# Moving side work in a fused attention and MLP kernel: weight signs in halves, one norm later, one y block a step, weight sums at the heads of steps

## The reference

```python
q = _l2norm(proj(Wq)); k = _l2norm(proj(Wk)); v = proj(Wv)
attn = jnp.einsum('bhqd,bhkd->bhqk', q, k)
mask = (rel < 0) | (rel >= WINDOW)              # rel = key - query, WINDOW = 128
bias = jnp.where(mask, NEG_INF, -abs(rel) * slopes)
attn = jax.nn.softmax(attn + bias, axis=-1)
out = einsum('bhqk,bhkd->bhqd', attn, v) @ Wo.T
x = _layernorm(x + out)                          # called y below
# MLP: bw = mean(|w|, axis=1) * sign(w)
h = gelu(x @ bw1.T + b1)
x = _layernorm(x + h @ bw2.T + b2)
```

## Time and profile before

| | |
|---|---|
| median of 3 runs | 389.81 us (389.2 to 392.25) |
| the profiled execution | 391.93 us, its span 390.2 us |
| granted TensorE clock, mean | 0.99 of full |
| busy: PE, DVE, ACT, POOL | 372.1, 303.2, 311.3, 273.9 us |

### The profile page before, as it was taken

How to read it: one execution, slowest core, us unless ns; L and a number is a source line. 1 busy time by engine, 2 the same in 40 slices (tenths; PEclk the granted TensorE clock), 3 DMA queues, 4 the chain that set the end, 5 groups by cost and what they waited for, 6 DMA issues and landing times.

```text
span 390.2 us, 12067 instructions
## 1 busy us (share of the span) xinstructions
PE 372.1 (95%) x3921; PEld 239.8 (61%) x3921; DVE 303.2 (78%) x856; ACT 311.3 (80%) x533; POOL 273.9 (70%) x418
## 2 busy tenths in 40 slices
PE   8788999999999999999999899999999999999992
PEld 5544665666566656665666556666666666666671
DVE  3965767776777677767777787765899999999985
ACT  2687788878887888788878878868998888888774
POOL 1185888888888888788877998869556646655221
PEclk9998999999999999999999999999999999999997
DMA  7596555653355335533553448420522124304113
GB/s 235 118 247 144 119 127 108 149 123 82 81 121 120 82 81 120 121 81 81 122 119 82 82 85 134 83 55 5 54 55 55 55 55 110 89 19 108 55 54 108
DMA packets 98544, 38.30 MB, mean 98 GB/s; under 512 B 84688, under 2 KB 97360, under 8 KB 98256
## 3 DMA queue, kind: packets, MB, share of 16 engines
q1 hardware_dynamic: 98512, 37.89, 44.1%
HBM read 12.72 MB, written 4.19 MB: 43 GB/s over the span
## 4 chain that ended last, share of the span: by engine, by line
PE 78%; DVE 8%; issue 4%; ACT 3%; POOL 2%; DMA 2%; SPq 1%; DVEq 0%; POOLq 0%; ACTq 0%
PE ps L506 14%; PE ps L377 13%; PE ps L540 13%; PE ps L366 12%; PE ps L348 8%; PE ps L388 6%; PE ps L411 6%; PE ps L396 3%; PE ps L403 2%; DVE ss L894 1%; DMA qkT<-parts 1%; POOL parts L1263 1%; PE ps L451 1%; ACT prob L639 1%; POOL prob L1243 1%
## 5 line engine op out<-in xcount | busy, mean ns | idle before, releaser
L1243 POOL TENSOR_SCALAR_AFFINE_SELECT prob<-prob 128x512 f32<-128x512 f32 x252 | 153.5, 644 | 19.4 <-ACT prob L639 19.4
L639 ACT ACTIVATE prob<-ps 128x1024 f32<-128x1024 f32 (+1 forms) x128 | 123.0, 1014 | 0.4 <-PE ps L348 0.3
L377 PE MATMUL ps<-wqkv,xt 128*128 128x512 f32 x128 | 72.9, 657 | 1.9 <-DVE qkn L911 1.9
L506 PE MATMUL ps<-yT,sgn 128*128 128x512 f16 x256 | 61.2, 379 | 0.0
L540 PE MATMUL ps<-sgn,prob 128*128 128x256 f16 x512 | 60.6, 273 | 0.2 <-DVE prob L1042 0.2
L705 ACT ACTIVATE ps<-ps,bias,alpha 128x512 f32<-128x512 f32 x64 | 47.7, 754 | 13.3 <-PE ps L506 10.3
L540 PEld LDWEIGHTS ps<-sgn,prob 128*128 128x128 f16 x512 | 50.0, 98 | 12.2 <-DVE prob L1042 0.5
L1309 POOL TENSOR_TENSOR resid<-z,resid 128x256 f32 (+1 forms) x31 | 22.5, 726 | 45.1 <-DVE z L1052 45.1
L366 PE MATMUL ps<-prob,vdiag 128*17 128x128 f32 x1024 | 51.2, 274 | 1.6 <-POOL prob L1243 1.6
L366 PE MATMUL ps<-prob,vnext 128*17 128x128 f32 x992 | 49.8, 273 | 0.0
L843 DVE COPY parts<-parts 128x512 f16<-128x512 f16 x32 | 19.7, 615 | 35.0 <-POOL parts L1263 34.9
(11 more groups left out here) (108 smaller groups left out, 580.5 us busy)
## 6 DMA issues: line engine op xcount, KB each, us to landing
xt<-in_xT SPq DMA_DIRECT2D x32, 128.0 KB, 2.4
resid<-in_x SPq DMA_DIRECT2D x32, 128.0 KB, 2.3
out_dram<-resid SPq DMA_DIRECT2D x7, 512.0 KB, 3.0
w_t<-in_w2T SPq DMA_DIRECT2D x1, 1024.0 KB, 7.9
w_t<-in_w1T SPq DMA_DIRECT2D x1, 1024.0 KB, 6.5
w_nat<-in_w SPq DMA_DIRECT2D x4, 256.0 KB, 3.6
wqkv<-in_wqkvT SPq DMA_DIRECT2D x3, 256.0 KB, 3.9
qkT<-parts SPq DMA_TRANSPOSE x32, 4.3
```

The source lines that it names most:

```text
L377: mm = nc.tensor.matmul(ps[:, QK[1 - par], :], xt[:, slot, k, :], wqkv[:, k, 0:2 * D], start=(k == 0), stop=(k == DC - 1))
L506: mm = nc.tensor.matmul(ps[:, bank, :], sgn1[:, c, P * k:P * k + P], yT[:, par, a, c, :, :], start=(m == 0), stop=(m == 2 * DC - 1))
L639: nc.scalar.activation(to, scored, ACT.Exp, scale=QK_SCALE ** -2).then_inc(exp_done, 1)
L1243: return nc.gpsimd.affine_select(out=at, in_=at, compare_op=ALU.is_ge, fill=0.0, base=-near, pattern=[[0, CH], [1 if near else -1, P]], ch ...
```

## The change

Nothing is computed differently. On ACT, `signs1` becomes two halves of 128 x 1024 in the asides of steps 2 and 3, behind exponential 3, and waits for the w1T load alone. `norm_of(0)` leaves the end of step 0 and stands in step 1 behind exponential 1. The first group's four high_y go one each into steps 24 to 27; the second group's go one each into 28 and 29, and two into 30. In step 29 the high halves move from behind exponential 1 to behind exponential 3. On POOL the first group's four low_y go one each into steps 24 to 27, ahead of the low halves. On DVE `fade_values(1, 1)` leaves step 1 and stands in step 0 ahead of the Newton round of block 3; the second 128 columns of the w2 sums become two pieces of 64 at the very heads of steps 2 and 3; the w1 sums and the two bound pieces move from the asides to the heads of steps 24 to 27, ahead of the doubling copy. On SP and PE the order is the same, only the semaphores that are waited for are renamed or counted anew (`turn_y(0, 0)` still stands between the transposes of blocks 28 and 29).

```diff
@@ sync
-            sp.dma_start(w1_t[:], w1T).then_inc(mlp_in, 16)
+            sp.dma_start(w1_t[:], w1T).then_inc(w1t_in, 16)
...
-                sp.dma_start(dst[:], src).then_inc(mlp_in, 16)
+                sp.dma_start(dst[:], src).then_inc(bias_in, 16)
@@ scalar: step()
                 exps(0)
                 exps(1)
-                if early2:
+                if amid:
+                    amid()
+                if high_behind == 1:
                     high_halves(i, par)
...
                 exps(3)
+                if high_behind == 3:
+                    high_halves(i, par)
                 if aside:
                     aside()
-                if next3 or prev3:
+                if norm and (next3 or prev3):
                     norm_of(i, next3, prev3)
...
-            def signs1():
-                act.wait_ge(mlp_in, 16 * 3)
-                nc.scalar.activation(sgn1[:], w1_t[:], ACT.Sign).then_inc(sgn_ready, 1)
+            def signs1(part):
+                act.wait_ge(w1t_in, 16)
+                nc.scalar.activation(sgn1[:, part], w1_t[:, part], ACT.Sign).then_inc(sgn_ready, 1)
...
-            step(0, 0, prev2=False, prev3=False, early2=True, both=False)
-            step(1, 1, prev2=False, prev3=False)
-            signs1()
-            step(2, 0, prev3=False)
-            step(3, 1)
+            step(0, 0, prev2=False, prev3=False, high_behind=1, both=False, norm=False)
+            step(1, 1, prev2=False, prev3=False, amid=lambda: norm_of(0, True, False))
+            step(2, 0, prev3=False, aside=lambda: signs1(0))
+            step(3, 1, aside=lambda: signs1(1))
...
-            step(NB - 8, 0, aside=lambda: high_pair(0))
-            step(NB - 7, 1, aside=lambda: high_pair(2))
-            step(NB - 6, 0, aside=lambda: high_y(1, 0, 1))
-            step(NB - 5, 1, aside=lambda: high_y(1, 1, 1))
-            step(NB - 4, 0, aside=lambda: high_y(1, 2, 1))
-            step(NB - 3, 1, next3=False, early2=True, aside=lambda: high_y(1, 3, 1))
-            step(NB - 2, 0, next2=False, next3=False)
+            step(NB - 8, 0, aside=lambda: high_y(0, 0, 0))
+            step(NB - 7, 1, aside=lambda: high_y(0, 1, 0))
+            step(NB - 6, 0, aside=lambda: high_y(0, 2, 0))
+            step(NB - 5, 1, aside=lambda: high_y(0, 3, 0))
+            step(NB - 4, 0, aside=lambda: high_y(1, 0, 1))
+            step(NB - 3, 1, next3=False, high_behind=3, aside=lambda: high_y(1, 1, 1))
+            step(NB - 2, 0, next2=False, next3=False, aside=high_pair)
@@ vector: step()
+                if ahead:
+                    ahead()
                 if cur and not next3:
                     fade_values(i, par)
                 if next1:
...
+            def second_block():
+
+                double(2, 0)
+                fade_values(1, 1)
...
-            step(0, 0, prev2=False, next1=False, prev3=False, prev4=False, aside=lambda: abs_w2(0),
-                 amid=lambda: double(2, 0))
-            step(1, 1, prev2=False, next1=False, prev3=False, prev4=False)
...
-            step(2, 0, prev3=False, prev4=False, aside=abs_w2_and_residuals)
-            dve.wait_ge(mlp_in, 16 * 3)
+            step(0, 0, prev2=False, next1=False, prev3=False, prev4=False, aside=lambda: abs_w2(0, P), amid=second_block)
+            step(1, 1, cur=False, prev2=False, next1=False, prev3=False, prev4=False)
+            step(2, 0, prev3=False, prev4=False, ahead=lambda: abs_w2(P, P + P // 2),
+                 aside=lambda: dve.wait_ge(first_resid, 16 * XS))
+            dve.wait_ge(bias_in, 16 * 2)
...
-            step(3, 1, prev4=False)
+            step(3, 1, prev4=False, ahead=lambda: abs_w2(P + P // 2, D))
...
-            step(NB - 8, 0, aside=lambda: abs_w1(0))
-            step(NB - 7, 1, aside=lambda: abs_w1(1))
+            step(NB - 8, 0, ahead=lambda: abs_w1(0))
+            step(NB - 7, 1, ahead=lambda: abs_w1(1))
...
-            step(NB - 6, 0, aside=bound_sides)
-            step(NB - 5, 1, aside=bound_rows)
+            step(NB - 6, 0, ahead=bound_sides)
+            step(NB - 5, 1, ahead=bound_rows)
@@ gpsimd
+                if before_low:
+                    before_low()
                 if next2 and not early2:
                     low_halves(i, par)
...
-            for b in range(GB):
-                step(NB - 8 + b, b % 2)
-                if b < 2:
-                    low_y(0, 2 * b, 0)
-                    low_y(0, 2 * b + 1, 0)
+            step(NB - 8, 0, before_low=lambda: low_y(0, 0, 0))
+            step(NB - 7, 1, before_low=lambda: low_y(0, 1, 0))
+            step(NB - 6, 0, before_low=lambda: low_y(0, 2, 0))
+            step(NB - 5, 1, before_low=lambda: low_y(0, 3, 0))
```

More of the change, by code:

```diff
@@ L622, in take_rows, with step @@
                                      ACT.Copy).then_inc(ot_ready, 1)
-            def step(i, par, prev2=True, next2=True, next3=True, prev3=True, early2=False, both=True,
-                     rows_first=False, aside=None):
+            def step(i, par, prev2=True, next2=True, next3=True, prev3=True, high_behind=None, both=True,
+                     rows_first=False, norm=True, amid=None, aside=None):
                 if prev2:
@@ L938, in _, with abs_w2 @@
             nc.vector.tensor_copy(vnext[:, :, HD], fade[:, 1, :]).then_inc(consts, 1)
-            def abs_w2(part):
-                cols = slice(part * P, part * P + P)
+            def abs_w2(first, last):
+                cols = slice(first, last)
                 dve.wait_ge(w2_in, 16)
```

26 lines of the change are left out of this document (12 added, 14 removed).

## The result

| | before | after |
|---|---|---|
| median of the runs | 390.00 us (9 runs) | 388.27 us (9 runs, 387.05 to 388.76) |
| the profiled execution, its span | 391.93, 390.2 us | 388.27, 386.4 us |
| ratio of the times | | 0.9945 (0.9925 to 0.9965) |

The medians differ by 1.7 us (0.44%); the ratio of all the runs says 0.55%, with an interval of 0.35 to 0.75%. The forecast was 382.8 us, a gain of 7, in a range of 381.0 to 386.0. The two profiled executions differ by more than the medians do, 3.7 against 1.7 us; that difference is the first thing to explain.

A forecast was written before the change was run, and what follows sets the result against it. PE was taken as the bound, so only overlong steps could give: 0.9 + 3.70 - 0.2 + 2.68 - 0.2 + 0.4 = 7.3 us; carried to the median 382.5, named 382.8 us, range 381.0 to 386.0.

The forecast's parts named there:

- What bounds the kernel: PE is busy throughout a plain step of 7.75 or 7.76 us; only longer steps can give anything.
- Signs in halves: Step 2 falls from 11.45 to 7.75 us: gain 3.70, of which 1.57 strips wait and about 1.7 half clock.
- The first rival: Step 2: the clock falls all the same, or didn't in the median's runs; 1.7 us not gained, 384.5; chance 0.12.
- Norm of block 3: Step 1: exponentials and masks start earlier, gain 0.9 us (0.54 to 1.22); later qkn of block 3 costs 0.
- The landing: Start of step 3: transpose of block 3 lands at 36.5, close to need; charged 0.2 us, bounds 0 and 0.5.
- w2 pieces: Heads of steps 2 and 3: each piece fits DVE's 1.38 us wait for POOL's low halves; cost 0, bound 0.3.
- w1 sums, high_y, low_y: Steps 25 and 26 return to 7.76 us: gain 1.64 + 1.04 = 2.68 us, lower bound 1.06.
- The contention: Step 25: low_y beside DVE's Newton round delays the w1 sum; charged 0.2 us, bounds 0 and 1.1.
- the second rival: Side work only moves its stall: sign halves hold norms, or y transpose holds block 29's; either 384.6 us; chance 0.15.
- Step 29: High halves behind exponential 3 end PE's 0.68 us wait for oT; gain 0.4 us, bounds 0 and 0.68.
- SP and the y transpose: End of step 27: transpose of y ready about 3.5 us later, closer to block 29's; taken as 0.
- the signs of being wrong: qkT wait at step 3 or 29, otok wait in 3 or 4, clock 0.50 past 20 us, slow Newton operations in 24-27.

The follow-up runs named there:

- norm_back: The changed kernel with the norm of block 3 back at the end of step 0 and the fades back in step 1: 388.04 us, ratio 0.9927.
- before_again: The unchanged kernel from before the change, measured and profiled once more: 390.26 us, ratio 1.0002.
- late_only: Kernel before with only the late half of the change (y, w1 sums, bounds, step 29); steps 0 to 3 as before: 389.28 us, ratio 0.9970.
- high_first: The changed kernel with ACT's high halves of block 3 ahead of the norm of block 4 in step 1: 388.22 us, ratio 0.9942.

## Why the prediction was wrong

*What bounds the kernel.* Right: PE does, and step 26 fell to 7.79 us, step 2 in norm_back to 7.75.

Two steps of it failed, each by about 1.8 us: the size of the signs' term, and the cost of the moved norm, which was put at 0. A third, the landing of block 28 in step 27, was no term at all and cost 0.9.

*Signs in halves, 3.70 us.* The mechanism was right (the wait for strips is gone), but the size came from one execution: "about 1.7 the half clock" was in the profiled run of before and not in its usual one (9.69 against 11.45 us). The gain to be had was 1.94 us by before_again, and 1.45 by late_only, where the bias load came sooner. The first rival, which said just this, was given 0.12. The sign was in the numbers: the profiled execution lay 2.1 us above the median, and the text carried that over as a constant, but for 0.3 us, instead of asking which term it was in. The Trainium skill (TensorE: Matmul & The Clock Gate, Part 1) says that the monitor behind the clock runs free of the kernel's start, so that a fall comes at other places in other runs; the two profiles of one kernel agree, 0.50 and 1.00 in the same half microsecond.

*Norm of block 3: gain 0.9, cost 0.* The gain was about right (0.74 us). "Cost 0" failed as a mechanism. It argued that the high halves wait for the norm of block 4 anyway, and took that norm's time as given; but its seed stands on DVE behind the Newton round that was moved, and the move put the round beside POOL's masks, 1.75 us for its three operations instead of about 0.6. The cost was 0.86 us by the wait for otok and its like (step 2 at 8.61 or 8.62 where block 3 lands in 4.6 us, against 7.75). Where it lands slowly, step 2 is 9.60 us against 8.29 with the norm back: 1.31. No run took POOL's masks away from that round alone; that they make it late is read from the timelines. The landing was charged 0.2 us, with the transpose assumed 0.7 us earlier; it was issued 0.8 us later. Of the 1.94 us that the halves give, almost nothing is left: step 2 is 9.60 against 9.69 us.

*w2 pieces, cost 0.* Right in after, for want of something early to delay, and just right in norm_back (the piece ends at 30.92, POOL's low halves at 30.88); in high_first the piece took 1.06 us ahead of the doubling.

*w1 sums, high_y, low_y: 2.68 us.* Steps 25 and 26 gave 1.06 and 1.01. The contention was seen, and charged at 0.2 us with 1.1 as its bound; it took 0.57 us of PE's time. The Trainium skill (GPSIMD Engine Reference, Specifications) would have had all three operations slowed; the trace has two of three with one low_y beside them (0.68, 0.20, 0.71; the second fell into a gap of POOL's) and all three with two (0.68, 0.59, 0.60). The other 0.9 us were given back in step 27: steps 25 and 26 had been a cushion for block 28, whose slow landing was in the trace of before and hidden. The forecast looked for a late landing of block 29 and not of block 28. That is the second rival ("side work only moves its stall"), by another transpose than it named.

*Step 29: 0.4 us.* Right, 0.37. *SP and the y transpose: 0.* Right; it landed in 3.8 us where it had taken 6.3.

Of the signs of being wrong that the prediction named, two came: PE's wait for qkT at the start of step 3, and Newton operations of 0.6 to 0.7 us in step 24 with a wait for otok behind them.

The sum against the usual before: 0.74 in step 1, 0.09 in step 2, 2.07 in steps 25 and 26, less 0.92 in step 27 and 0.08 in 28, 0.37 in 29, less 0.1 in 30, is 2.2 us; the medians say 1.7.

## What to carry to other kernels

A profile is one execution: when it lies above the median, find the term that makes it so before any term of a sum is read from it, and don't price a fall of the clock that one profile shows. When an instruction moves, read again the duration of what it triggers at its new place, beside its new neighbours (here a small DVE operation lasted until the POOL instruction beside it ended), and follow the engine's order behind it, not only its reader. When stalls are removed, look in the steps behind them for transfers that those stalls had hidden.
